# Attention scores of a two-layer transformer block: from packed bf16 parts over 96 rows, reloaded from DRAM, to fp32 matmuls over 32 rows, four heads in four row groups

## The reference

```python
# layer 0, modulated by cond (shift, scale, gate from silu(mod) @ w_ada)
h = ln(x) * (1 + sc) + sh
q, k, v = split(roll(h @ w_qkv, -64))          # 8 windows of 128 tokens a batch
scores = einsum('bnqhd,bnkhd->bnhqk', q, k) / 4
x = x + gate * (roll(softmax(scores) @ v, 64) @ w_so)          # attention 1
q = h @ w_q;  k, v = split(context @ w_kv)     # 154 context tokens
scores = einsum('bqhd,bkhd->bhqk', q, k) / 4
top_s, top_i = top_k(scores, 16)               # 16 best of 154, softmax over those
x = x + gate * ((softmax(top_s) @ v[top_i]) @ w_co)            # attention 2
x = x + gate * ((silu(h @ w_a) * (h @ w_b)) @ w_m2)            # MLP, 256 -> 2 x 1024 -> 256
# layer 1
x = x + softmax(q @ k.T / 4) @ v @ sa_wo + t_sa                # attention 3, 1024 x 1024 scores a head
x = x + softmax(where(mask, q @ kc.T / 4, -inf)) @ vc @ ca_wo + t_ca   # attention 4, 154 masked tokens
x = x + gelu(h @ w1) @ w2 + t_mlp                              # MLP, 256 -> 1024 -> 256
```

## Time and profile before

| | before |
|---|---|
| median of 3 runs | 1883.4 us (1880.19, 1883.4, 1887.14) |
| profiled execution, its own time | 1880.98 us |
| span of that execution, first to last instruction | 1878.9 us |
| mean granted clock of TensorE | 0.847 of full speed |
| PE, busy | 1371.0 us, 73% |
| DVE, busy | 1006.3 us, 54% |
| ACT, busy | 776.6 us, 41% |
| POOL, busy | 307.1 us, 16% |
| DMA | 115851 packets, 103.65 MB |

### The profile page before, as it was taken

One profiled execution on the slowest core, in us unless ns is written; L12 is line 12 of the kernel. 1 busy time (PEld: TensorE's weight loads), 2 busy tenths in 40 slices (PEclk: granted clock), 3 DMA queues, 4 the chain that ended last, 5 costly groups with the idle time before them and its releaser, 6 DMA issues.

```text
span 1878.9 us, 22617 instructions
## 1 busy us (share of the span) xinstructions
PE 1371.0 (73%) x7052; PEld 697.2 (37%) x7052; DVE 1006.3 (54%) x2985; ACT 776.6 (41%) x1626; POOL 307.1 (16%) x518
## 2 busy tenths in 40 slices
PE   2746557464556677756678989999879977778988
PEld 1324345332334334433333424322422214333556
DVE  4444335465776555565476556777777715643120
ACT  0213224244554445434123544566546673444221
POOL 7010010324444322232310000100010000100110
PEclk9958778675556989877699989999999998888999
DMA  4496873203111011012910031252313021440000
GB/s 159 147 162 141 134 126 82 43 26 78 22 22 25 1 22 22 1 40 81 129 18 1 1 55 48 77 100 29 45 43 46 13 42 22 87 65 6 12 15 23
DMA packets 115851, 103.65 MB, mean 55 GB/s; under 512 B 25115, under 2 KB 95504, under 8 KB 115476
## 3 DMA queue, kind: packets, MB, share of 16 engines
q1 hardware_dynamic: 114844, 101.82, 28.6%
q10 hardware_dynamic: 887, 0.39, 0.1%
HBM read 69.95 MB, written 31.63 MB: 54 GB/s over the span
## 4 chain that ended last, share of the span: by engine, by line
PE 38%; DVE 9%; issue 4%; DMA 2%; ACT 2%; SPq 2%; POOL 1%; ACTq 0%; DVEq 0%; POOLq 0%
PE bank L811 6%; PE bank L782 6%; PE bank L746 5%; PE ring L708 5%; PE ring L725 5%; DVE part_max L1200 3%; PE ring L661 2%; PE ring L685 2%; DVE x_hat L1174 1%; ACT pr L1003 1%; PE bank L814 1%; PE bank L816 1%; PE bank L752 1%; DMA ks<-ctx_mask 1%; PE ring L692 1%
## 5 line engine op out<-in xcount | busy, mean ns | idle before, releaser
L1003 ACT ACTIVATE pr<-bank 128x512 f32<-128x512 f32 x656 | 366.2, 596 | 259.7 <-PE bank L782 191.0
L1200 DVE TENSOR_REDUCE part_max<-bank 128x1 f32<-128x512 f32 x512 | 325.0, 684 | 169.5 <-PE bank L746 168.5
L746 PE MATMUL bank<-ks,qs 96*128 96x512 bf16 x512 | 197.4, 393 | 35.9 <-DVE part_max L1200 27.0
L782 PE MATMUL bank<-qs,ks 100*128 100x512 bf16 x512 | 195.0, 387 | 27.7 <-ACT pr L1003 16.0
L842 PE MATMUL bank<-ident,probs 128*128 128x128 f32 x256 | 58.5, 370 | 130.8 <-POOL probs L1339 130.6
L1234 DVE MAX8 top<-bank 128x8 f32<-128x154 f32 x256 | 69.9, 314 | 133.2 <-PE bank L831 133.0
L811 PE MATMUL bank<-pr,vs 128*32 128x512 f32 x1024 | 137.7, 610 | 1.0 <-ACT pr L1003 1.0
L1020 ACT ACTIVATE exp_all<-bank,neg 128x154 f32<-128x154 f32 x256 | 85.1, 387 | 111.3 <-POOL neg L1328 110.5
L708 PE MATMUL ring<-h_t,w_m 128*128 128x512 f32 x256 | 131.0, 639 | 0.0
L782 PEld LDWEIGHTS bank<-qs,ks 100*128 100x128 bf16 x512 | 48.3, 97 | 215.1 <-ACT pr L1003 159.0
L1273 POOL TENSOR_SCALAR var_eps<-mean_var 128x4 f32<-128x4 f32 x24 | 5.8, 241 | 729.3 <-DVE mean_var L1165 728.9
(11 more groups left out here) (153 smaller groups left out, 2275.6 us busy)
## 6 DMA issues: line engine op xcount, KB each, us to landing
qs<-q_dram SPq DMA_DIRECT2D x192, 128.0 KB
q_dram<-parts SPq DMA_DIRECT2D x32, 384.0 KB, 2.5
ks<-k_dram SPq DMA_DIRECT2D x96, 128.0 KB
v_dram<-v_out SPq DMA_DIRECT2D x32, 256.0 KB, 2.9
vs<-v_dram SPq DMA_DIRECT2D x16, 512.0 KB
k_dram<-parts SPq DMA_DIRECT2D x16, 384.0 KB, 2.6
w_m<-in_L_xcond_w_m SPq DMA_DIRECT2D x1, 2048.0 KB, 9.7
w_m<-in_L_xcond_w_m SPq DMA_DIRECT2D x2, 1024.0 KB, 6.4
```

The source lines that it names most:

```text
L746: last = nc.tensor.matmul(bank[:, :], qs[0:PACK, h, t * P:(t + 1) * P], ks[0:PACK, h, kc * 512:(kc + 1) * 512], start=True, stop=True)
L782: last = nc.tensor.matmul(bank[:, :], ks[0:FULL, h, kt * P:(kt + 1) * P], qs[0:FULL, h, qc * 512:(qc + 1) * 512], start=True, stop=True)
L1003: nc.scalar.activation(m.pr[:, u % NPR, :], m.bank[2 + u % 2][:, :], ACT.Exp).then_inc(m.s_free, 1)
L1200: nc.vector.tensor_reduce(m.part_max[:, slot, i // 2, i % 2:i % 2 + 1], bank[:, :], axis=AX.X, op=ALU.max).then_inc(m.m_read, 1)
```

## The change

What it does:

- **fp32 over 32 rows.** The projections are copied from PSUM into SBUF tiles that stay there ("slots", [128, 2, 1024] fp32). Each copy is made twice: once with the odd heads multiplied by zero and once with the even ones, so that a 32-row group holds one head's 16 rows and 16 of zeros. The two copies are made by ScalarE (`qk_a`) or VectorE (`qk_d`), unit by unit in turn. A score matmul is fp32 over 32 rows, and four heads of a group lie in four row groups of the array. The m matmuls take their heads in the order 2, 3, 0, 1, the s matmuls in the order 0, 1, 2, 3, one of each in turn. The maximum is one fp32 row in the padding, written by one DMA without a split. Values stay in SBUF, 17 columns a head.
- **Gone:** the bf16 split, the stores and `load_qk`/`load_v`, the nine constants of GpSimd at the start, and their like later. The context's keys and values for layer 1 are written to DRAM once and loaded back once.
- **Banks.** `banks_of` says which banks a step may use; `Plan.finish` takes an empty one, and where none is empty it moves the step that empties one (its follow-up) ahead. m and s share 3 to 6; scores of the top-k attention have 2, 3 and 4, its transposes 5 and 6; token stages 0, 1 and 2 (0 and 1 beside the top-k); value products 7.
- **Order.** `W` goes 8 to 13 (attention 1), 60 to 56 (attention 3, lead of the maxima 0.0625 to 0.1), 14 to 12 (attention 4, whose first maxima move into attention 3's last group). The step that empties a bank stands one place later in the token stages. Top-k runs half a batch's tiles of each group at a time, its score matmuls 1.6 instead of 1.2 steps ahead; the attention's output is transposed and divided for half a group at a time. x is loaded in four pieces a batch, and the mask's arithmetic comes after the statistics. Attention 4 has 12 m units a group for 11, and its tails one matmul over the whole array.

The diff, cut to its core:

```diff
+def banks_of(step):
+
+    kind = step[0]
+    if kind in ("m", "m_turn", "s"):
+        return (3, 4, 5, 6)
+    if kind == "c_score":
+        return (2, 3, 4)
+    if kind == "c_turn":
+        return (5,)
+    if kind == "c_tail":
...
+        placed, last, turn = set(), {}, {}
+        self.steps, self.bank, self.before = [], {}, {}
+        for step in waiting:
+            if step in placed:
+                continue
+            banks = banks_of(step)
+            if banks:
+                empty = [x for x in banks if x not in last or follow_up(last[x]) in placed]
+                bank = min(empty or banks, key=lambda x: turn.get(x, -1))
+                if not empty:
+                    follow = follow_up(last[bank])
+                    self.steps.append(follow)
+                    placed.add(follow)
+                    self.moved.append((follow, step))
+                self.bank[step] = bank
+                self.before[step] = last.get(bank)
+                last[bank], turn[bank] = step, len(self.steps)
+            self.steps.append(step)
+            placed.add(step)
...
-def group_run(plan, a, start, width, lead, ready):
+def group_run(plan, a, start, width, lead, late):
...
-    W = 8.0
...
+    W = 13.0
...
-    W = 60.0
...
+    W = 56.0
...
-    end = group_run(plan, 3, A3, W, 0.0625, A3 + 3.6 * W)
...
+    end = group_run(plan, 3, A3, W, 0.1, 2.6)
...
-    W = 14.0
...
-    end = group_run(plan, 4, A4, W, 0.4, A4 + 3 * W)
...
+    W = 12.0
+    A4 = end + 2 - W
+    end = group_run(plan, 4, A4, W, 0.4, 1.6)
...
             elif at == 3:
-                h, t, kc = i // 16, i // 2 % 8, i % 2
-                last = nc.tensor.matmul(bank[:, :], qs[0:PACK, h, t * P:(t + 1) * P], ks[0:PACK, h, kc * 512:(kc + 1) * 512], start=True, stop=True)
+                t, kc, h = i // 8, i // 4 % 2, (i + 2) % 4
+                if i == 0:
+                    for n in range(2):
+                        for signal in g.projected(gi, n, (0, 1)):
+                            pe.wait_ge(*signal)
+                k, rows = m.k_of[at, b, gi % GB], slice(HW * h, HW * h + HW)
+                last = nc.tensor.matmul(bank[:, :], q[rows, t * P:(t + 1) * P], k[rows, kc * 512:(kc + 1) * 512], start=True, stop=True)
...
             elif at == 3:
                 qc, kt, h = i // 32, i // 4 % 8, i % 4
-                last = nc.tensor.matmul(bank[:, :], ks[0:FULL, h, kt * P:(kt + 1) * P], qs[0:FULL, h, qc * 512:(qc + 1) * 512], start=True, stop=True)
+                k, rows = m.k_of[at, b, gi % GB], slice(HW * h, HW * h + HW)
+                last = nc.tensor.matmul(bank[:, :], k[rows, kt * P:(kt + 1) * P], q[rows, qc * 512:(qc + 1) * 512], start=True, stop=True)
...
-            if v < 2:
-                pe.wait_ge(m.m_read, plan.n("m_turn", 7) + 1)
-            else:
-                pe.wait_ge(m.left1_done, 2 * (v - 1))
-                pe.wait_ge(m.all_done, v - 1)
...
+            r = 2 * (gi % 2) + hf
+            rows = slice(HW * r, HW * r + HW)
             for hh in range(2):
-                h = 2 * hf + hh
-                last = nc.tensor.matmul(m.bank[v % 2][:, hh * C:hh * C + S2], m.qs[gi % 3][0:PACK, h, t * P:(t + 1) * P],
-                                        m.ks2[:, gi % 2, h, 0:S2], start=True, stop=True)
+                last = nc.tensor.matmul(bank[:, hh * C:hh * C + S2], m.q2[b][rows, u, t * P:(t + 1) * P], m.kc[rows, u, hh, b, :], start=True, stop=True)
...
-        elif kind == "hi":
...
-            nc.scalar.activation(m.parts[:, i % 2, 0, :], g.bank("qk", s, b, n, u)[:, :], ACT.Identity, bias=qk_bias(s, u)).then_inc(m.hi_done, 1)
...
+            else:
+                name, factor = padded_names(s, u)
+                c = MARKS.index(factor + "0")
+                for odd in range(2):
+                    last = nc.scalar.activation(place_of(m, s, b, n, u, odd), g.bank("qk", s, b, n, u)[:, :], ACT.Identity,
+                                                bias=m.padded[:, name, odd, u % 2:u % 2 + 1], scale=m.marks[:, c + odd:c + odd + 1])
+                last.then_inc(g.free("qk", s, b, n, u), 1)
...
+        elif kind == "qk_d":
...
+            for odd in range(2):
+                last = nc.vector.tensor_scalar(place_of(m, s, b, n, u, odd), g.bank("qk", s, b, n, u)[:, :], m.marks[:, c + odd:c + odd + 1],
+                                               m.padded[:, name, odd, u % 2:u % 2 + 1], ALU.mult, ALU.add)
+            last.then_inc(g.free("qk", s, b, n, u), 1)
...
-    for i in range(3):
-        nc.gpsimd.memset(m.qs[i][PACK:FULL, :, :], 1.0).then_inc(m.fills, 1)
-        pool.wait_ge(m.fills, 3 + 3 * i)
-        nc.gpsimd.memset(m.ks[i][PACK:FULL, :, :], 1.0).then_inc(m.fills, 1)
-        pool.wait_ge(m.fills, 4 + 3 * i)
-        nc.gpsimd.memset(m.ks[i][PACK:PACK + 1, :, :], 0.0).then_inc(m.fills, 1)
-        pool.wait_ge(m.fills, 5 + 3 * i)
...
-            for r in range(len(Q_PART)):
-                sp.dma_start(m.qs[slot][r * D:(r + 1) * D, :, :], m.q_dram[at][Q_PART[r], r0:r0 + HG * D, :].rearrange("(h d) t -> d h t", d=D)
-                             ).then_inc(m.qk_in[slot], 16)
...
         elif kind == "max_rows":
             gi = step[1]
-            i, slot = plan.order[step], gi % 3
-            sp.wait_ge(m.max_split, i + 1)
-            sp.wait_ge(m.consts, 2 if gi >= 16 else 1)
-            for part in range(3):
-                sp.dma_start(m.qs[slot][MAX_ROW + part:MAX_ROW + part + 1, :, :].rearrange("o h t -> o (h t)"),
-                             m.max_parts[:, i % 2, part, :]).then_inc(m.max_in[slot], 16)
+            i = plan.order[step]
+            sp.wait_ge(*g.freed("m_turn", gi))
+            sp.dma_start(m.q_of[attention(gi), batch_of(gi), gi % GB][MAX_ROW[gi % 2]:P:HW, :], m.max_sb[:, i % 2, :]).then_inc(m.max_in[i % 2], 16)
```

1268 lines of the change are left out of this document (598 added, 670 removed).

## The result

The changed kernel takes 2423.16 us (2408.54 to 2437.82, 3 runs) against 1883.4: 1.287 times the time before, 95% interval [1.277, 1.298]. I had forecast 1665, and the range ended at 1860.

The account below looks back on a forecast made before the run. No engine was full over the span (TensorE 73%); bounds differed by stage, waits in some, TensorE nearly full in full attention. Terms summed to -217 from 1878.9, giving 1662, stated as 1665 us; eight-in-ten range 1540 to 1860.

Parts of the forecast that it names:

- rival C: Full attention of layer 1: clock falls to half as TensorE waits a fifth of each set; +204, 1869 us; chance 0.08.
- D: Score matmuls: row groups do not overlap at all; full attention +483, other attentions +80, 2230 us; chance 0.08.
- A: Full attention of layer 1 does not slow, 3.7 us a set; 1581 us in all; chance 0.18.
- B: Top-k loop stays, its wait moving to transposes or ScalarE; stage keeps 550 us, 1810 in all; chance 0.10.
- E: Row groups overlap only between neighbouring matmuls, 0.43 us apiece, a set 4.9 us plus tokens; +128, 1793 us; chance 0.06.
- Start: Before the first maxima: constants, mask arithmetic, bf16 split and first DMA round trip go; -54 us.
- Attention 1: Windowed attention of layer 0, 110:330: waits for keys go, fp32 units add +40 of TensorE work; -45, for 175 us.
- Top-k: Top-k attention, 330:910: VectorE's wait for scores goes; from 580 to 405 us, floor 330; -175.
- 910:1000: Stretch before full attention's s matmuls: four banks for the maxima and no DMA wait; -15 us.
- Attention 3: Full attention of layer 1, 1000:1562: sets without tokens lengthen from 3.31 to 4.45 us; +84 us.
- Attention 4: 1562:1735: first maxima move earlier, -20; fp32 maxima and tails add about 35 to TensorE's 134; -8 in all.
- Last MLP: 1735:1879: same matmuls, TensorE 131 us busy, evacuations ordered later; -4 us.

Follow-up runs that it names:

- heads apart: Changed kernel with the m matmuls taking their heads two places later, so that neighbours lie in different row groups: 1926.15 us, 1.025 of before.
- the run with two banks: Kernel with the m matmuls' heads moved two places later, with two banks instead of three for the top-k scores: 2031.53 us.
- the three runs with other numbers of rows: Attention 3's score matmuls over 128 rows in the changed kernel: 2350.98 us; over 32 or 64 rows in the kernel before: 2035.77 and 1995.69 us.

## Why the prediction was wrong

**The step that failed** is "Four column groups thus run at once. I take row groups to do the same". They do, when neighbours lie in different row groups; that these neighbours do was never looked up. The code's offset of two heads suggests it, but the plan has each maximum beside a score two places on, and the two cancel. So only two matmuls ran at once, and a set that I had reckoned at 4.45 us took 5.66 at the full clock and 10.11 at half. The heads in the plan's order could have been written out before any run. Second, rival C had the right event with the wrong cause: "After, TensorE waits a fifth of each set", so I took idleness for the danger. It fell to half with TensorE 100% busy, and stayed up in the kernel with heads apart that waits 13%. C and D, at 0.08 each, both came, each in part. A and B did not: attention 3 got slower, and the top-k did not keep its 550 us. E, overlap between neighbours only, falls by the trace: s0 streams beside s3 with m3 between them in the order, and with heads apart a set took 4.58, not 4.9.

**Term by term**, against the stages of before, in us:

- Start: -54 forecast, first maxima at 50 for 109, -59. Right.
- Attention 1: -45 forecast, 283 (50 to 333) against 225 (109 to 334), +58. The 1024 passes of L777 and L818 were sized at 96 us; the page gives 84.9 and 87.0, and since the two lines overlap in part, together they keep TensorE busy for 144.56 us of 50:333. Units overlapped little, and the clock of 0.74 was left out of that number. That is 49 us of the 98 by which TensorE was busier than my 176 (274.12 of the 283 us). The start is a part of the rest: the modulation matmuls, over by 81 and so ahead of the first maxima before, now run from 70 to 111, behind them. In all the top-k began where it had begun before.
- Top-k: -175 forecast, 574 to 435, -139. Mechanism right: VectorE's own work is 323.37 against a floor of 330, its wait for scores before the first maxima search is 42.6 us on the page for 133.0 before, and the run with two banks shows that the third does most of it. The stage ended 30 us above my 405. (TensorE's 425 us would be 308 at the clock of 1000:1562, not 300; nothing hangs on it.)
- 910:1000: -15 forecast, 98 and 98, 0. Why nothing was gained there no run settles.
- Attention 3: +84 forecast, +612. Of this, 1168 - 714 = 454 are the row groups and the clock that fell with them; the 45 sets of 10.11 instead of 5.66 are 200 of it by themselves. The rest, 158, is what fp32 over four row groups costs when it works: +89 in the middle 72 sets (forecast +76), +11 in the last 16 (forecast +3), and +58 in the first 40 (forecast +5; with my own 5.85 and 5.75 it should have read +4). That +89 and +76 are close is in part luck: my 3.75 was the mean of 72 sets at 3.93 and 16 at 2.76, so my 4.8 a set stood for +63 only, and the sets took 5.17. Amid tokens the waves cost far more than I took. My reading is that a token matmul takes the whole array and the next wave must wait for it; no run tests that.
- Attention 4: -8 forecast, 173 to 228, +55. I had TensorE busy for 35 us more than its 134; it was busy for 216.31. The maxima's passes (L797 busy 90.2 us on the page) overlapped little, and the clock was 0.79.
- Last MLP: -4 forecast, 144 and 144, 0.

Sum: -59 + 58 - 139 + 0 + 612 + 55 + 0 = 527, and the spans differ by 2406.8 - 1878.9 = 527.9.

In the kernel with heads apart, with the clock up in attention 3, the time is still 2.5% above before: of the 165 us gained until its first value product (1006 to 841) attention 3 takes 158, and attention 4 another 47 (220 for 173).

## What to carry to other kernels

Before counting on concurrent row groups, write out which row group each neighbour in TensorE's order uses, across the streams that a plan interleaves: four matmuls of 32 rows run at once only when four different groups stand next to each other, with four free banks. Read the clock row beside the busy row: a TensorE that is 100% busy with a part of its rows can run at half speed, and a denser, even a longer, program can be the faster one. A bank added where nothing else runs is a gain; shared with another stream it can give the gain back.

## What the runs showed of the hardware

- A wave of four fp32 matmuls over 32 rows and 512 columns takes 1.15 us from 1419.49 to 1420.64, where one after the other they take 4 x 0.86 = 3.44: 3.0 times. The Trainium skill ("TensorE: Matmul & The Clock Gate", Part 3, Measured speedup vs the span model) gives 3.07; the runs agree.
- A matmul can start ahead of one that precedes it in another row group: s0 at 1837.28, m3 at 1839.15. The Trainium skill (same page, Part 3, The mechanism) says that matmuls start and end strictly in program order. For the starts the trace shows the contrary; for the signals of their ends it agrees, as the exponential at 1841.14 shows.
- The reach of this can be short. At this place of attention 1, with heads apart, a unit is eight passes of one row group, and the unit behind it starts only when five of these have started, 0.55 us after the first:

```profile
239.74 0.82 PE L818 MATMUL bank<-slot 32*128 32x128 f32 x5
240.29 0.37 PE L777 MATMUL bank<-slot 32*128 32x128 f32 x1
```

- The granted clock stood at half for 100 us (1860:1960) without any idle time of TensorE, and at full with the same busy share over the whole array. By the Trainium skill (same page, Part 1: The HAM clock gate) the gate follows how busy TensorE has been; read as "a matmul is running", the three runs with other numbers of rows contradict it.
- A set cost 10.11 / 5.66 = 1.79 times as much at half clock with two at once, 5.39 / 3.30 = 1.63 with bf16. It is less than 2, since evacuation does not slow down with TensorE: an exponential takes 0.60 us at half clock (1839.39) as before the change.
